# Step and input rows of a feature pair side by side, one transfer a ring slot, and gates read ahead of the rows' writes

## The reference

```
h = tokens(x)
h = h + ssm(norm(h))            # selective state space scan, 16 states a feature
h = h + moe(norm(h))            # 8 experts of width 768, top 2
h = h + bimamba(norm(h))        # down to 96, a scan forward and a scan backward, back up to 192
h = h + moe_dense(norm(h))      # 8 experts of 192 x 192, top 2, weighted by softmax gates
```

```
state[t] = decay[t] * state[t-1] + step[t] * u[t] * B[t];   y[t] = sum over states of state[t] * C[t]
decay[t] = exp(step[t] * A)
```

## Time and profile before

| | us |
|---|---|
| median of 3 runs | 964.87 |
| lowest, highest run | 955.78, 965.11 |
| span of the profiled execution | 959.2 |

### The profile page before, as it was taken

The page is one execution under the profiler, slowest core; times in us unless marked ns, Lnnn a source line. Parts: engine busy times, 40 slices in busy tenths (PEclk is TensorE's granted clock), DMA queues, the critical chain, the costliest instruction groups (busy, mean ns, idle before and its releaser), DMA issues. The chain is left out here.

```text
span 959.2 us, 11504 instructions
## 1 busy us (share of the span) xinstructions
PE 741.7 (77%) x3608; PEld 587.3 (61%) x3608; DVE 564.3 (59%) x968; ACT 403.8 (42%) x876; POOL 395.1 (41%) x311
## 2 busy tenths in 40 slices
PE   7877887784647879887999568797769986986756
PEld 5645656553437879787899346565556764663534
DVE  4167779679675613312112587888877787789320
ACT  1548374282225224322345356373617352733110
POOL 1045745665663321321003244653538333834503
PEclk8899999797667989999999789988978999897978
DMA  9469655355585567877676778697688657967211
GB/s 349 134 211 337 206 158 143 100 148 145 144 232 150 164 193 237 262 234 232 212 232 191 196 195 223 173 239 182 153 220 218 153 141 222 240 151 191 79 61 37
DMA packets 84668, 179.51 MB, mean 187 GB/s; under 512 B 12740, under 2 KB 32832, under 8 KB 83840
## 3 DMA queue, kind: packets, MB, share of 16 engines
q1 hardware_dynamic: 79776, 171.55, 63.3%
q0 software_dynamic: 4832, 7.24, 2.6%
HBM read 158.02 MB, written 20.69 MB: 186 GB/s over the span
## 5 line engine op out<-in xcount | busy, mean ns | idle before, releaser
L1670 PE MATMUL PS<-PR,CM 128*128 128x304 f32 (+1 forms) x672 | 186.3, 419 | 92.7 <-POOL PR L790 63.8
L790 POOL TENSOR_TENSOR PR<-ST,V 128x608 f32<-128x608 f32 x96 | 142.3, 1482 | 185.7 <-DVE ST L1304 155.5
L1670 PEld LDWEIGHTS PS<-PR,CM 128*128 128x128 f32 x672 | 126.5, 220 | 135.7 <-POOL PR L790 77.7
L956 ACT ACTIVATE dA<-dA,negA 128x304 f32<-128x304 f32 x192 | 93.6, 538 | 151.8 <-DMA BB<-rows_d 151.7
L1304 DVE TENSOR_TENSOR_SCAN ST<-dA,PS 128x608 f32<-128x608 f32 x96 | 136.3, 1420 | 15.1 <-ACT dA L956 10.9
L1008 ACT ACTIVATE HID<-PS,WX 128x128 f32<-128x128 f32 x204 | 59.5, 367 | 149.7 <-PE PS L1670 147.6
L703 POOL TENSOR_TENSOR dA<-dA,aP 128x607 f32<-128x607 f32 x48 | 70.7, 1475 | 73.1 <-ACT aP L976 71.2
L1293 DVE TENSOR_TENSOR PS<-BB,PS 128x608 f32<-128x608 f32 x96 | 76.2, 794 | 22.5 <-DMA BB<-rows_d 11.3
L1500 DVE TENSOR_TENSOR xp<-PS,WXB 128x192 f32<-128x192 f32 x34 | 12.2, 358 | 128.2 <-PE PS L1670 123.4
L1670 PE MATMUL PS<-XT,WX 128*128 128x128 f32 x408 | 84.1, 290 | 1.0 <-ACT HID L1008 1.0
L1670 PE MATMUL PS<-XT,WXR 128*128 128x128 f32 x408 | 83.8, 289 | 0.0
(11 more groups left out here) (363 smaller groups left out, 1287.8 us busy)
## 6 DMA issues: line engine op xcount, KB each, us to landing
dA<-rows_d SPq DMA_DIRECT2D x144, 304.0 KB
BB<-rows_d SPq DMA_DIRECT2D x144, 304.0 KB
WX<-ex_m SPq DMA_DIRECT2D x34, 576.0 KB
WX<-ex_m SPq DMA_DIRECT2D x34, 387.0 KB, 3.8
slots_d<-WXR SPq DMA_DIRECT2D x8, 960.0 KB, 8.2
WXR<-ex_r SPq DMA_DIRECT2D x34, 192.0 KB, 4.6
WX<-gates_d SPq DMA_DIRECT2D x4, 1216.0 KB, 6.3
CM<-c SPq DMA_DIRECT2D x1, 4430.0 KB, 19.6
```

Source lines behind the costliest of these rows:

```text
L790: nc.gpsimd.tensor_tensor(PRq[:, c % 2], STq[:, c % 2], DIRS[k].Cw.unsqueeze(1).broadcast_to([128, QB, T]), ALU.mult).then_inc(q_product.s ...
L956: last = nc.scalar.activation(dAq[:, slot, i, :], dAq[:, slot, i, :], ACT.Exp, scale=negA[:, j:j + 1])
L1670: return nc.tensor.matmul(out, lhsT, rhs, start=first, stop=last)
```

## The change

- `rows_d` becomes `[2, 96, 2, 2, T]`: direction, pair of neighbouring features, kind, feature of the pair, t. The step rows and input rows of a pair are side by side, 4 x 304 elements.
- `dA` and `BB` become one buffer `RING` with, in each slot, kind 0 and then kind 1. `fill_slot` is one transfer of 608 KB with runs of 4,864 bytes, where it was two of 304 KB with runs of 2,432; a slot's landing counts 16 and not 32. The first pass uses the same functions. The buffer of gathered rows, `GA0`, lies in the ring's first bytes.
- `write_gates(g-1)` moves from behind the last ring read of a backward pass to between the reads of c10 and c11; `read_gates(g-1)` moves from behind `write_rows(g+1, 0)` to before it. DVE's `gates_rows` moves from n = 7 to n = 6, behind the scan of c6.

```diff
-        dAK, BBK = (sb(x, [128, SLOTS * QB * T]) for x in ("dA", "BB"))
+        RING = sb("RING", [128, SLOTS * 2 * QB * T])
...
+        ring = RING[:, :].rearrange("p (a k b t) -> p a k b t", a=SLOTS, k=2, b=QB)
+        dAq, BBq = ring[:, :, 0], ring[:, :, 1]
...
-        rows_d = nc.dram_tensor("rows_d", [2, 2, D, T], fp32, kind="Internal").ap()
+        rows_d = nc.dram_tensor("rows_d", [2, D // QB, 2, QB, T], fp32, kind="Internal").ap()
...
+            def write_kind(k, kind, x, signal):
+
+                rows = rows_d[k, :, kind, :, :]
+                sp.dma_start(rows[0:DM // QB], x[:, 0:T]).then_inc(signal.sem, 16)
+                sp.dma_start(rows[DM // QB:, :, 0:HALF], x[0:DR, T:PK]).then_inc(signal.sem, 16)
+                sp.dma_start(rows[DM // QB:, :, HALF:T], x[DR:128, T:PK]).then_inc(signal.sem, 16)
...
             def fill_slot(k, c, slot, signal):
 
-                for kind, ring in enumerate((dAq, BBq)):
-                    rows, per, j = rows_d[k, kind, 0:DM, :], MAIN_BLOCKS, c * QB
-                    if j >= MAIN_BLOCKS:
-                        rows, per, j = rows_d[k, kind, DM:D, :], REST_BLOCKS, j - MAIN_BLOCKS
-                    rows = rows.rearrange("(i j) t -> i j t", j=per)[:, j:j + QB, :].rearrange("i j t -> i (j t)")
-                    sp.dma_start(ring[:, slot].rearrange("p b t -> p (b t)"),
-                                 rows.unsqueeze(0).broadcast_to([NS, FB, QB * T])).then_inc(signal.sem, 16)
+                rows = rows_d[k].rearrange("q k b t -> q (k b t)")
+                rows, per, j = rows[0:DM // QB], MAIN_BLOCKS // QB, c
+                if c >= per:
+                    rows, per, j = rows_d[k].rearrange("q k b t -> q (k b t)")[DM // QB:], REST_BLOCKS // QB, c - per
+                rows = rows.rearrange("(i j) n -> i j n", j=per)[:, j, :]
+                sp.dma_start(ring[:, slot].rearrange("p k b t -> p (k b t)"),
+                             rows.unsqueeze(0).broadcast_to([NS, FB, 2 * QB * T])).then_inc(signal.sem, 16)
...
                     if c == 8 and g >= 2:
                         store(g - 2)
+                    if c == QSTEPS - 2 and g:
+                        write_gates(g - 1)
                     if c == QSTEPS - 1 and g >= 2:
                         store_end(g - 2)
                 if g:
-                    write_gates(g - 1)
+                    read_gates(g - 1)
                 if g + 1 < GROUPS:
                     write_rows(g + 1, 0)
-                if g:
-                    read_gates(g - 1)
...
+                    if n == 6 and tail is not None:
+                        gates_rows(Q, tail, Q_BANK)
                     if n == 7:
-                        if tail is not None:
-                            gates_rows(Q, tail, Q_BANK)
```

## The result

The changed kernel took 971.22 us (median of 13 runs, 962.79 to 977.03) against 965.63 us for the kernel before (13 runs, 955.78 to 972.30): a ratio of 1.0077, 95% interval 1.0052 to 1.0103. I had forecast 951.5 us. The profile after has a span of 971.1 us.

The account below looks back on a forecast made before the run. From about 533 us on, PE's expert products and DVE's scans were taken to bound the kernel, with late ring landings holding DVE in places. Nine terms sum to 13.4 us: 964.9 - 13.4 = 951.5 us, range 943 to 961.

Parts of the forecast that it names:

- The pace of a slot: Ring trains: a slot filled by one transfer takes 2.0 us instead of 2.46, bounds 1.7 to 2.46.
- The terms at passes 4 to 7: DVE's waits behind late ring slots shrink: -1.9 us in pass 4, -1.7 in pass 5, -0.7 and -1.0 in 6 and 7.
- Passes 8 to 11 elsewhere: nothing: Passes 8 to 11 outside the places priced: PE's mixture products set the end, so no gain from the ring.
- The slower rival: Ring trains: long runs move worse; at 2.9 us a slot 14 us lost, less the gates' 7: 972 us; chance 0.10.
- Boundaries: Starts of the forward passes of groups 2 and 3: gates read ahead of the rows' writes, -3.0 and -1.2 us.
- The smaller danger that I named: Boundaries: the new order shows the rows' landing; two us of delay would turn the -4.2 to nothing.
- a sign of being wrong that I had named: Boundaries: a new wait of SP on the gates' write that pushes the rows' writes back; no size given.
- Tail: After the last scan: GpSimd's 2.96 us wait for group 2's gates goes, -2.9 us, bounds 1.5 to 2.96.
- The rival of a fixed part in each transfer: Ring transfers: a fixed part goes with the second transfer, 4 to 6 us more gain, 946 us; chance 0.07.
- Gates' part as a whole: Gates' terms at the two boundaries and the tail together: 3.0 + 1.2 + 2.9 us of gain.
- The only-the-gates rival: Ring keeps 254 GB/s; only the gates' terms and 0.3 us of issues remain: 7.4 us gain, 957.5 us; chance 0.21.
- DVE's copy: Gates' copy L1248 (0.43 us) one step up, behind scan c6: 1.24 us to spare, so no cost to DVE.

Follow-up runs that it names:

- the ring alone: Kernel without the tower, SyncE only filling the ring in trains of different transfer forms: 252 GB/s for the old form, 230 for the new, 407 for one row to all.
- the ring's part: Kernel before with only the new row layout and the single transfer a slot, gates at their old places: 973.88 us, ratio 1.0115.
- the gates' part: Kernel before with only the gates moved (copied at n = 6, written between c10 and c11, read ahead of the rows' writes): 960.61 us, ratio 0.9971.

## Why the prediction was wrong

- **The pace of a slot** is the step that failed: 2.0 us taken, 2.75 measured, outside my bounds of 1.7 to 2.46 on the bad side. I put the long run near the gate reads, because they too copy the same bytes to all partitions. The larger of them does it with one level of 128; the ring has 16 by 8, and the ring alone shows one row for all at 407 GB/s and the ring's form at 230. My ceiling, "no gain", ruled out a loss for which I had a rival but no row. A row that spoke for it was there: a full share at only 254 GB/s, against 367 for the loads, was a sign that this transfer was limited by its form, and the form was what the change altered.
- **The terms at passes 4 to 7** had their places right: the same waits moved, but up, from 2.29, 0.92 and 4.47 to 2.93, 3.08 and 5.32. Instead of -6.3 us the ring's part made the stretch 9.9 us longer alone, and 10.7 beside the gates' part (369.4 against 358.7). "Passes 8 to 11 elsewhere: nothing" failed too: from first to last scan passes 8, 10 and 11 were 1.1, 1.4 and 2.3 us longer than before, and with the ring's part alone 0.8, 1.4 and 0.8, so a slower ring costs there too.
- **The slower rival** had the mechanism: longer runs move worse, decided from 2.7 us a slot on. At 2.75 it came to +5.6 us; its price of +7 (14 less the gates' 7) was worked out at 2.9. Its own sum at the measured pace, 32 slots x 0.30 = 9.6 us, is close to the 9.9 and 10.7 by which the stretch grew. I gave it 0.10 because "both other rates" were higher; both belong to another form of transfer.
- **Boundaries**, -3.0 and -1.2: in the changed kernel, from the memset that ends `steps` to the first scan, 16.1 us for 18.8 at pass 8 (-2.7), and 16.1 for 15.9 at pass 10 (+0.2). The order went as planned at pass 8: gate reads issued at 708.41, row writes from 710.50. The smaller danger that I named, rows' landing shown instead of hidden, is what kept the rest: ring reads at 720.52, 6.1 us behind the last row write's issue. At pass 10 a sign of being wrong that I had named came true as well. SyncE stood on the gates' write (issued at 801.46), its gate reads ran over the memset, and the rows' writes went out 0.8 us behind it, where before they followed at once (797.75 and 797.84):

```profile
806.57 0.33 SPq L646 DMA_DIRECT2D WX<-gates_d  x1
806.95 1.40 SPq L650 DMA_DIRECT2D WX<-gates_d  x2
808.40 0.68 SPq L499 DMA_DIRECT2D rows_d<-q_DL  x1
```
```profile
807.56 0.07 DVE L1368 MEMSET q_DL<- 128x12 f32 x1
```

- **Tail**, -2.9: the wait fell from 2.96 to 0.99, -2.0. The gates' write of the changed kernel was seen 4.7 us after its issue there, where I took 3.5, and 4.9 us at the first boundary, where I took 4.
- **The rival of a fixed part in each transfer** has no support: with one level and different rows, two transfers a slot went at 392 GB/s and one at 407, so 1.59 and 1.53 us a slot.
- **Gates' part as a whole**: -7.1 forecast, -4.5 by these places (2.7 - 0.2 + 2.0), -2.8 by the ratio of the kernel with it alone. The only-the-gates rival, at 957.5 us, kept the ring's old pace; that kernel ran at 960.6.
- **DVE's copy** moved a step up cost nothing, as said: its only wait in the profile is the 0.9 us that it had before.
- What stays open: why 4,864-byte runs are slower than 2,432-byte ones in the two-level form (228 against 257, and 245 against 285 without sharing). The drift of engines past each other is only argued.

## What to carry to other kernels

Before making a transfer's runs longer, compare its GB/s at a full DMA share with that of plain loads in the same trace: if it is far below, its form may be what limits it, and then neither the count of transfers nor the run length is the cost to go for. Price a new transfer by a row with the same levels of source and destination, not by one that only carries similar bytes. And where a large read sits at a boundary, moving it to the other side of a small write moves the delay with it; a signal for each part that its reader takes brought the time to 0.9% below the kernel before, where the reordering alone brought 0.3%. With a second issuing engine, whose next step waits for the same data, it was 1.2 to 1.4%, though the runs do not show the second engine's share by itself.

## What the runs showed that I had not expected

A source with levels 16 by 8 fills 128 partitions at 228 to 262 GB/s with all 16 DMA engines busy when its rows are shared, and at 245 and 285 when they are not; one with a single level does it at 392 to 407, shared or not. Within the two-level form shorter runs are faster (230 at 4,864 bytes, 262 at 2,432), and at 1,216 the issue seems to be the limit (240 GB/s at a share of 0.86: four issues of 0.6 us are 2.4 us of the 2.6 a slot took). The Trainium skill's page "DMA: Bandwidth & Descriptors", section "🎯 Rules for kernel authors", advises to coalesce many small transfers into one, and names under 64 KB as mostly overhead; at 304 KB a transfer this case goes the other way, by 10 and 14% (252 and 262 GB/s against 230). The same section of the Trainium skill says that spreading transfers over issuing engines gives no bandwidth and only saves issue time. The traces agree on the first, 243 GB/s from two engines for 257 from one; for the second, the two gaps were 3.4 us less in the profile where the rows' issue was split (4.98 to 2.44, 6.35 to 5.47), though that one profile ran shorter than its kernel's median (949.33 us for 958.78).
